# Score tiles on column quarters and 32 by 32 block turns on VectorE for every second query tile

## The reference, cut to what matters

```python
x = x + conv(gather(group_norm(x)))            # (8, 128, 56, 56): 8 images of 3136 tokens, 128 channels
t = to_tokens(x)
# attention on the tokens of each image, causal, one head of 128, all in fp32
q, k, v = (einsum('btc,hc->bth', ln(t), W) for W in (Wq, Wk, Wv))
scores = where(causal, einsum('bth,bsh->bts', q, k) * C ** -0.5, -inf)
t = t + einsum('bts,bsh->bth', softmax(scores, axis=-1), v)
t = t + expert_layer(ln(t))                    # the 8 best tokens of each of 64 experts
```

## Time and profile before

| | us |
|---|---|
| median of 3 runs | 2917.45 |
| lowest and highest | 2912.93 and 2919.99 |
| the profiled execution | 2912.74 |
| its span, first to last instruction | 2910.8 |
| PE busy (records of matmuls) | 2692.5 (93%) |
| DVE busy | 1887.0 (65%) |
| ACT busy | 1786.9 (61%) |
| mean share of full TensorE clock | 0.972 |

### The profile page before, as it was taken

How to read it: one execution, slowest core, us unless ns; L and a number is a source line. 1 busy time by engine, 2 the same in 40 slices (tenths; PEclk the granted TensorE clock), 3 DMA queues, 4 the chain that set the end, 5 groups by cost and what they waited for, 6 DMA issues and landing times. The chain is left out here.

```text
span 2910.8 us, 53258 instructions
## 1 busy us (share of the span) xinstructions
PE 2692.5 (93%) x18974; PEld 2108.2 (72%) x18974; DVE 1887.0 (65%) x7229; ACT 1786.9 (61%) x4118; POOL 1757.3 (60%) x1837
## 2 busy tenths in 40 slices
PE   5688999999999999999999999999999998999775
PEld 3466787778777887778777887778777886787543
DVE  3467665867577665867577666867587656665324
ACT  3455666666676676666676676666676666665420
POOL 5777775776477756775477756775477656730000
PEclk8799999999999999999999999999999999999897
DMA  6445334633265324633265324633354323422397
GB/s 185 119 148 138 113 111 130 165 109 103 81 161 143 107 82 132 164 111 97 88 163 139 108 82 134 162 116 91 95 158 146 104 85 106 122 55 91 112 398 306
DMA packets 220067, 382.71 MB, mean 131 GB/s; under 512 B 44425, under 2 KB 130377, under 8 KB 219291
## 3 DMA queue, kind: packets, MB, share of 16 engines
q0 software_dynamic: 89856, 255.58, 30.1%
q1 hardware_dynamic: 125787, 108.75, 12.5%
q10 hardware_dynamic: 4160, 14.98, 1.3%
HBM read 316.77 MB, written 62.39 MB: 130 GB/s over the span
## 5 line engine op out<-in xcount | busy, mean ns | idle before, releaser
L533 POOL DMA_INDIRECT shared<-pair_table,idx x1800 | 1733.7, 963 | 833.0 <-issue 527.6
L1145 PEld LDWEIGHTS bank_o<-vals,prob_t 128*128 128x128 f32 x5200 | 633.7, 192 | 130.3 <-ACT prob_t L580 65.3
L1145 PE MATMUL bank_o<-vals,prob_t 128*128 128x128 f32 x5200 | 662.2, 276 | 31.5 <-ACT prob_t L580 31.5
L580 ACT ACTIVATE prob_t<-bank_r 128x512 f32<-128x512 f32 (+3 forms) x728 | 383.7, 548 | 474.1 <-PE bank_r L1132 473.3
L835 DVE CUSTOM_DVE_ANT_0 prob<-bank_r,mask 128x512 f32<-128x512 f32 (+3 forms) x728 | 449.2, 628 | 303.9 <-PE bank_r L1123 301.6
L1123 PE MATMUL bank_r<-keys,qt 128*128 128x512 f32 (+3 forms) x1456 | 635.7, 553 | 0.0
L825 DVE SCALAR_TENSOR_TENSOR shared<-shared,wb 128x128 f32<-128x128 f32 x1800 | 516.8, 347 | 163.8 <-ACT shared L561 163.0
L561 ACT ACTIVATE shared<-shared,wa 128x128 f32<-128x128 f32 x1800 | 561.6, 392 | 46.5 <-DMA shared<-pair_table,idx 46.5
L1112 PEld LDWEIGHTS bank_r<-convw_t,smp_t 128*128 128x128 f32 x3600 | 446.0, 195 | 56.5 <-issue 36.2
L1112 PE MATMUL bank_r<-convw_t,smp_t 128*128 128x128 f32 x3600 | 479.1, 279 | 1.1 <-ACT smp_t L566 1.1
L1132 PE MATMUL bank_r<-ident,prob 128*128 128x128 f32 x2600 | 383.1, 274 | 13.8 <-ACT prob L658 13.8
(11 more groups left out here) (158 smaller groups left out, 2198.2 us busy)
## 6 DMA issues: line engine op xcount, KB each, us to landing
shared<-in_dram SPq DMA_DIRECT2D x32, 1024.0 KB, 17.9
shared<-pair_table,idx POOLq DMA_INDIRECT x1800
pair_table<-rows_out SPq DMA_DIRECT2D x112, 256.0 KB
t<-in_dram SPq DMA_DIRECT2D x48, 256.0 KB, 4.1
t_dram<-t SPq DMA_DIRECT2D x48, 256.0 KB
shared<-in_dram SPq DMA_DIRECT2D x7, 1568.0 KB
stage<-t_dram POOLq DMA_DIRECT2D x8, 832.0 KB, 8.0
pm_dram<-logit SPq DMA_DIRECT2D x8, 800.0 KB
```

The source lines that it names most:

```text
L533: pool.indirect_dma_start(g[t % RING][:, n, :], None, pair_table[b % 2], bass.IndirectOffsetOnAxis(ap=idx[:, b % 2, i * TAPS + n:i * TAPS ...
L580: act.activation(prob_t[q % 3][:, 0:w], ring_bank(("prob", t, c))[:, 0:w], ACT.Copy)\
L1145: last = pe.matmul(attn_ps, prob_t[q % 3][:, n * P:(n + 1) * P], vals[:, slot(tb, at), :], start=(at == 0), stop=(at == ti))
```

## The change

Ten of the 25 query tiles of each image, those with 6, 8, 10, ... 24 key tiles (WIDE), are computed in another way. The rest, with 1 to 5 or an odd number of key tiles, stay as they were.

- **Scores.** For each chunk PE issues 16 products instead of one: four groups of 32 queries by four sets of keys (key blocks of 32, every fourth belongs to a set). The four sets go to the four column quarters. The scores of query group n and key set m land on partitions 32m to 32m+31, in the n-th quarter of the bank's columns.
- **Maximum.** DVE takes a maximum for each query group (L894 of the new file) after it has added the mask in PSUM in the last chunk (L893). It no longer copies the scores; ACT copies them to `prob` (`copy_scores`, L625). Since a query's keys are spread over four partitions, DVE's maximum over chunks (L1019) is turned by PE (`cross`, L1246), reduced over the four by DVE (L1029), sent back to all partitions by PE (`back`, four products, L1253) and copied by DVE (L949).
- **Exponential.** ACT needs four instructions, one for each query group, since the maximum differs (L706).
- **Turning.** DVE turns the chunk in 32 by 32 blocks straight from `prob` to `prob_t` (`turn_blocks`, L908). PE's 128 by 128 transposes and ACT's copies are gone for these tiles.
- **Sum.** For all tiles the row's sum now comes out of PE: the values have a 129th column of ones, and `attend` (L1267) multiplies 129 columns. ACT's sum with the exponential is gone. `attended` is counted at every chunk.

```diff
+BLK = 32
+BLKS = P // BLK
+WIDE = frozenset(range(5, TILES, 2))
@@ scores(c)
+                    if is_wide(ts):
+                        bank, cols = ring_bank(("score", ts, c)), w // BLKS
+                        sets = key_chunk(tb, k0, w).rearrange("p (j i k) -> p i j k", i=BLKS, k=BLK)
+                        for n in range(BLKS):
+                            for m in range(BLKS):
+                                last = pe.matmul(bank[m * BLK:(m + 1) * BLK, n * cols:(n + 1) * cols].rearrange("q (j k) -> q j k", k=BLK),
+                                                 qt[k % 2][:, at + n * BLK:at + (n + 1) * BLK], sets[:, m], start=True, stop=True)
+                        last.then_inc(scored, 1)
+                        return
@@ cross and back, on PE
+                    after(wide_max, wide_before(ts + 1))
+                    pe.transpose(ring_bank(("cross", ts, 0))[0:BLKS, 0:P], wmax[:], ident[:]).then_inc(cross_mm, 1)
...
+                    after(crossed, wide_before(v + 1))
+                    for m in range(BLKS):
+                        last = pe.matmul(ring_bank(use)[m * BLK:(m + 1) * BLK, 0:BLKS], neg[:], ident[0:BLKS, 0:BLKS],
+                                         start=True, stop=True)
@@ keep_scores and turn_blocks, on DVE
+                if is_wide(t):
+                    bank = ring_bank(("score", t, c))[:, 0:w].rearrange("p (b k) -> p b k", b=BLKS)
+                    if c == chunks_in(t) - 1:
+                        link(dve.tensor_tensor(bank[:, :, w // BLKS - BLK:], bank[:, :, w // BLKS - BLK:], mask_wide, ALU.add))
+                    dve.tensor_reduce(cmax[t % 2][:, c, :], bank, AXX, ALU.max).then_inc(score_ev, 1)
+                    return
...
+                after(exp_done, t + 1)
+                after(attended, q - 2)
+                dve.transpose(prob_t[q % 3][:, 0:w].rearrange("p (j b q) -> p b j q", b=BLKS, q=BLK),
+                              prob_blocks(t, k0, w).rearrange("p b (j k) -> p b j k", k=BLK)).then_inc(prob_ev, 1)
@@ the exponential, on ACT
-                    act.activation(row, row, ACT.Exp, bias=nmax[r][:, 0:1], accum_out=total[r][:, 0:1])\
-                       .then_inc(exp_done, 1)
+                    if is_wide(v):
+                        after(score_copied, wide_scores_before(v + 1))
+                        rows = prob_blocks(v, 0, (v % TILES + 1) * P)
+                        for k in range(BLKS):
+                            last = act.activation(rows[:, k, :], rows[:, k, :], ACT.Exp, bias=nmax[r][:, k:k + 1])
@@ attend(c)
-                        last = pe.matmul(attn_ps, prob_t[q % 3][:, n * P:(n + 1) * P], vals[:, slot(tb, at), :],
+                        last = pe.matmul(bank_o[:, 0:P + 1], prob_t[q % 3][:, n * P:(n + 1) * P], vals[:, slot(tb, at), :],
```

More of the change, by code:

```diff
@@ L145, with is_wide, wide_before @@
     CHUNKS_BEFORE.append(CHUNKS_BEFORE[-1] + chunks_in(_t))
+def is_wide(t):
+    return 0 <= t < ALL and t % TILES in WIDE
+def wide_before(t):
+    return sum(is_wide(u) for u in range(t))
 def rows_of(step):
@@ L166, in ring_order @@
         ts, v = step - LAG_S, step - LAG_V
+        if is_wide(v):
+            order.append(("back", v, 0))
         if step < ALL:
@@ L174, in ring_order @@
         order += misc_at(step, "F")
-        order += [("prob", v, c) for c in range(min(chunks_in(v), 2))]
+        turned = 0 if is_wide(v) else chunks_in(v)
+        order += [("prob", v, c) for c in range(min(turned, 2))]
         for c in inner_rounds(step):
-            order += [("prob", v, c + 1)] if c + 1 < chunks_in(v) else []
+            order += [("prob", v, c + 1)] if c + 1 < turned else []
             order += [("score", ts, c + 2)] if c + 2 < chunks_in(ts) else []
             order += misc_at(step, "M") if c == 1 else []
+        if is_wide(ts):
+            order.append(("cross", ts, 0))
         order += misc_at(step, "L")
@@ L662, in _ @@
                         keep_samples(step, p)
+                for c in range(min(chunks_in(step - LAG_S), 3)):
+                    copy_scores(step - LAG_S, c)
                 for use in misc_at(step, "E"):
@@ L990, in free_ring @@
                         after(score_ev, CHUNKS_BEFORE[t] + n + 1)
+                        if is_wide(t):
+                            after(score_copied, wide_scores_before(t) + n + 1)
+                    elif what == "cross":
+                        after(crossed, wide_before(t + 1))
+                    elif what == "back":
+                        after(max_done, t + 1)
                     elif what == "conv":
@@ L1163, in _ @@
                     fill_misc(use)
-                if chunks_in(v):
+                turned = 0 if is_wide(v) else chunks_in(v)
+                if turned:
                     turn_prob(0)
@@ L1482, in shape_constants @@
     mask = np.zeros((P, CHUNK + P), np.float32)
-    mask[:, CHUNK:] = np.where(np.arange(P)[None, :] > np.arange(P)[:, None], NEG, 0.0)
+    row, col = np.arange(P)[:, None], np.arange(P)[None, :]
+    mask[:, CHUNK - P:CHUNK] = np.where(col > row, NEG, 0.0)
+    key, query = row // BLK * BLK + col % BLK, col // BLK * BLK + row % BLK
+    mask[:, CHUNK:] = np.where(key > query, NEG, 0.0)
     of = np.arange(P) // (C // GROUPS)
```

147 lines of the change are left out of this document (104 added, 43 removed).

## The result

| | us |
|---|---|
| kernel before, median of 4 runs beside it | 2918.72 |
| changed kernel, median of 4 runs (3063.92 to 3069.03) | 3066.36 |
| ratio, with its 95% interval | 1.051 (1.0491 to 1.0528) |
| the profiled execution, and its span | 3067.9, 3066.1 |
| mean share of full TensorE clock (before 0.972) | 0.961 |

What follows compares the result with a forecast made beforehand. PE's instruction stream was taken to bound the kernel, with DVE's work up to its last `add_second` as each step's second bound. PE -42 and DVE +100 gave +58 us, median 2975 us, 2% slower; range 2868 to 3085.

Steps and rivals of the forecast that it cites:

- PE's turns gone: 1200 PE transposes of key tiles removed at 0.110 us each, all in steps that turn a changed tile: -132 us.
- quarter products and changes of shape: PE's score products on four quarters, +13 us, and 352 changes of array shape at 0.09 us, +32 us.
- B step: The step after a changed tile's scores are computed, in which that tile is turned; 80 in all.
- the DVE term: Block turns ahead of DVE's `add_second` make the turning steps late: 12.6 us an image, +100 us.
- step 5: A turning step forecast to stay bound by PE, with DVE busy 8.99 us of 20.64.
- Step 14: A turning step forecast to stay bound by PE and get shorter.
- `cross` and `back`: PE's part in exchanging maxima: 28 us of records and shape changes plus 13 us waiting for DVE, +41 us.
- A steps: Steps in which the scores of a changed tile are computed; 80 in all.
- ACT at nothing: ACT's score copies moving into score steps, and its four-part exponential, were costed at nothing.
- The prediction's own test: Stated sign of being wrong, among others: steps computing changed tiles' scores grow by more than 1 us on average.
- ACT is last in A steps: Rival: ACT's extra 3.6 us in steps 0, 2 and 4 costs 36 us in all, 3010 us; chance 6%.
- The faster rival: DVE's turns run in its present waits, so only PE's terms count: 2875 us; chance 22%.

Runs made afterwards that it cites:

- e12: Kernel before with one 128 by 128 PE turn a chunk instead of up to four in the ten tiles, 880 turns fewer; 2827.55 us, 0.9685.
- e7: Changed kernel without the exchange of maxima between key sets and with one 32 by 32 block turned a chunk on DVE; 2904.16 us, 0.9955.
- e9: e7 with one full product for each score chunk in place of the 16 on quarters; 2868.58 us, 0.9831.
- e2: Changed kernel without the exchange of maxima between key sets, each partition taking its own maximum; 2967.42 us, 1.0164.
- e13: e9 with the small piece standing for a chunk's turn done by ACT at its old place instead of by DVE; 2827.51 us, 0.9687.
- e14: e9 with ACT copying only 32 columns of a changed chunk's scores from image 2 on and the exponential's input times zero; 2832.92 us, 0.9712.
- e5: Changed kernel with no tile computed in the new way, leaving the 129th column and what else holds for all tiles; 2919.95 us, 1.0005.
- e6: Changed kernel with ACT copying only 32 columns of a changed chunk's scores from image 2 on and the exponential's input times zero; 3070.48 us, 1.0525.

## Why the prediction was right or wrong

The ledger, each term with the runs that it is from:

| term | forecast | measured | from |
|---|---|---|---|
| PE's turns gone | -132 | -125 | e12, 92 for 97 |
| quarter products and changes of shape | +45 | +36 (45 by the starts of the records) | e7 to e9 |
| the exchange | +41, and 0.45 us of DVE's chain in a B step | +99 | change to e2 |
| block turns, cut down to 192 ns each | in +100 | +63 | e2 to e7 |
| block turns, the rest: their place and the 192 ns | in +100 | +41 | e9 to e13 |
| ACT's score copies | 0 | +36 | e9 to e14 |
| 129th column | +4 | +2, not told from 0 | e5 |
| sum | +58 | +152 (148 measured) | |

The first line is 92 / 97 x 132. That the sum comes within 4 us is a check and no proof: three lines lean on e9, each known to 8 us, the first is scaled up from another kernel, and the two lines of 41 and 36 were not taken out together. The exponential in four parts stays in e2, e7, e9, e13 and e14; the sum leaves little for it.

**Right.** The small sizes, each read from a neighbouring row: the turn at 0.69 us for 0.65, DVE's busy time 2105.2 for 2100, three quarter chunks at 2.76 us for 2.73. (Its working for 0.88, 1.08 - 0.27 + 0.11, gives 0.92; 0.87 was measured, so the value was better than its sum.) The +45 for quarters and changes of shape agrees with the 45 that the starts add up to, but the changes are nearly all of it, where it had 32, and the half chunks add nothing, where it had 8. That PE alone would gain and DVE's turns would eat more than the gain: 63 + 41 = 104 us, where the DVE term said 100. That step 5 stays PE's and gets shorter: PE is busy in all of its 18.17 us, and it is 2.2 us shorter on average (22 x 0.110 - 0.35 = 2.1 by the prediction's terms). Step 14, which was to go the same way, did not.

**The step that failed most: `cross` and `back`.** It took the exchange to cost PE 0.35 us of running, and 0.55 us of waiting in 3 A steps of 10 (its own parts, 0.27 + 0.28 - 0.1, make 0.45), and took for granted that DVE answers at once. Measured 99 us for 80 tiles, 1.2 us each. The wait for `wmax` and `neg` is what stands ahead of them in DVE's order, `add_second` and through it ACT's `scale_first`, up to 2.8 us in place of 0.28. It named the copy of the maximum as 0.45 us of DVE's chain, and didn't ask who waits for the copy: the exponential, behind it ACT's sample copies, behind them PE (step 14, 3.3 us). And 12 of the 14 waits of PE of more than 2.5 us in steps 25 to 199 were followed by a stretch at 1.2 GHz.

**The second: ACT at nothing, and A steps that don't grow.** The prediction's own test, A steps grown by more than 1 us on average, came out against it: 2.5 us. More than half of that is the exchange (e2), so this test failed mainly for the first reason. ACT at nothing failed too: 36 us with the rest out, though nothing in place (e6). The rival "ACT is last in A steps" said 36 us as well, and that agreement is luck: it had 4.5 us an image in steps 0, 2 and 4, and e14 gained 1.3 there.

**The third: where DVE's term would stand.** The ten B steps were to get 1.3 us longer in an image (3.9 for the eight, and by the same terms -2.1 for step 5 and -0.5 for step 14); they got 3.0 shorter, step 14 alone 3.5 longer and the eight together 4.3 shorter. The prediction took DVE's last `add_second` to be what ends a B step. From the second image on PE did not wait for it at the end of a single B step of the changed kernel, 15.4 us in all before. What the turns cost is paid earlier in the step, where PE's product waits for them (38.4 us, and 70.9 as soon as the exchange is moved), and at the end of the A steps behind it. So the +100 has the right size and the wrong place, and its agreement with 104 is partly luck.

**The faster rival** (2875 us) fell by its time, but half of its mechanism held: in the ten B steps DVE's idle time fell from 46.8 to 31.0 us an image, so 16 us of the new work went into what had been waits, and the turns did not make `add_second` late. It asked only whether DVE finds room, and not whether the turned chunk is ready when PE wants it.

What stays open: how much of the 99, the 41 and the 36 us is PE at 1.2 GHz and how much is waiting as such. No run separates them; the traces give upper bounds. In steps 25 to 199 the time at 1.2 GHz falls from 92 to 65 us with the exchange out (e2), from 47.8 to 20.5 from e9 to e13 and from 47.8 to 13.7 from e9 to e14, and half of each fall is the most that it can be worth: 14, 14 and 17 us. Nor does a run tell how the 41 us divide into the turns' place and what was left of their length.

## What to carry to other kernels

A step that sends a small result to another engine and back is not priced by its instructions but by what stands ahead of each of them in the three queues, and by who waits behind the last; follow all hops before giving it a size, above all a hop through the engine whose tail you already know to be late. Moving work from the busiest engine to a less busy one also moves the moment at which the result is ready; ask where in the new engine's order it stands. Taking out one suspect while another still holds the end gives nothing (products 3 us in place, 36 later; copies 0, then 36), so a suspect is acquitted only when it was taken out last as well as first. And when a run agrees with a forecast in its total, look at the steps in which it should have gained: here a rival's 36 us came true in other steps than its own.

## What the runs showed of the hardware

- DVE's block turn of 128x512 in fp32 from SBUF to SBUF takes 691 ns, of 128x256 426 ns, of 128x32 192 ns; its maximum over 32 keys each of 128x512 from PSUM 684 ns.
- Sixteen fp32 products of 32 weight columns and 128 columns on the four column quarters take as long as one of 128 by 512 when they stand in a row with others (0.87 and 0.86 us from start to start). The change to them and back costs about 0.24 us more, 0.09 at the start and 0.15 at the end of a group. The Trainium skill, "TensorEngine Tiling (Array Packing)", Key Properties, says that a change of the tiling mode drains TensorE; the trace is in line with that and gives it this size.
- A product of 129 columns in place of 128 costs nothing that can be measured (276 ns a record in e5 and in the kernel before; 1.0005 of its time).
- Of the 14 waits of PE of more than 2.5 us in steps 25 to 199 of the changed kernel, 12 were followed by a stretch at 1.2 GHz that began during the wait or within 1.5 us of its end, also well inside a busy kernel (the window of step 18, mean 0.75). Of the 51 waits of 1 to 2 us, 5 were.
